# Convolution blocks of 49 tiles instead of 56, three slots instead of two, and weighing two groups behind picking, in a four-layer graph network

## The reference

```python
# second layer, twice (r0, r1): the weight depends on the edge's type
x_src = x[src]
for r in range(8):
    msg = msg + jnp.where((edge_type == r)[:, None], x_src @ W[r], 0)
agg = segment_sum(msg * norm[:, None], dst)
out = agg + x @ root + bias

# fourth layer, three times (c0, c1, c2): the weight is a sum over 8 edge attributes and a constant
W = (edge_attr @ ew + eb).reshape(E, 16, 16)
agg = segment_sum(einsum('ei,eio->eo', x[src], W), dst)
out = agg + x @ rw + rb
```

## Time and profile before

| | us |
|---|---|
| runs | 14,904.42, 14,911.91, 14,941.55 |
| median | 14,911.91 |
| profiled execution | 14,959.53 |
| its span, first to last instruction | 14,958.3 |
| mean granted TensorE clock (share of full) | 0.744 |
| busy: VectorE / GpSimd / TensorE / ScalarE | 11,150.7 / 9,259.2 / 8,297.6 / 4,791.5 |
| share of the span: VectorE / GpSimd / TensorE / ScalarE | 75% / 62% / 55% / 32% |

### The profile page before, as it was taken

One profiled execution on the slowest core, in us unless ns is written; L12 is line 12 of the kernel. 1 busy time (PEld: TensorE's weight loads), 2 busy tenths in 40 slices (PEclk: granted clock), 3 DMA queues, 4 the chain that ended last, 5 costly groups with the idle time before them and its releaser, 6 DMA issues. The chain is left out here.

```text
span 14958.3 us, 147756 instructions
## 1 busy us (share of the span) xinstructions
PE 8297.6 (55%) x41291; PEld 5702.8 (38%) x41291; DVE 11150.7 (75%) x19230; ACT 4791.5 (32%) x2765; POOL 9259.2 (62%) x6976
## 2 busy tenths in 40 slices
PE   1222222222220688588836566665668858885886
PEld 0111111111110566466623233333356646663664
DVE  6999999999998566466635455554559967995996
ACT  0111111111110466456621001010037746773774
POOL 6777777777752466556655555555337756774776
PEclk5555555555555899789967777787779989997998
DMA  2444444444441222122211111111123323332332
GB/s 83 156 154 153 153 153 156 157 154 153 153 157 40 84 63 67 53 61 67 65 42 36 37 37 34 38 36 37 27 69 114 111 79 100 113 111 67 114 111 73
DMA packets 629773, 1371.10 MB, mean 92 GB/s; under 512 B 262833, under 2 KB 403118, under 8 KB 554126
## 3 DMA queue, kind: packets, MB, share of 16 engines
q1 hardware_dynamic: 405534, 1076.25, 20.0%
q0 software_dynamic: 224112, 293.30, 8.8%
HBM read 656.16 MB, written 712.80 MB: 92 GB/s over the span
## 5 line engine op out<-in xcount | busy, mean ns | idle before, releaser
L536 POOL DMA_INDIRECT h<-in_x,idx x1568 | 3051.7, 1946 | 1206.2 <-DMA efT<-in_edge_attr_t 785.3
L550 PE MATMUL PS<-waug,efT 17*128 17x256 f32 x6272 | 1129.4, 679 | 3167.2 <-DVE e L587 2179.1
L1681 PE MATMUL PS<-hot,lhs 128*128 128x392 bf16 x9408 | 1855.5, 355 | 1228.4 <-issue 762.8
L1668 POOL DMA_INDIRECT myg<-node_table,mix x1568 | 1662.6, 1060 | 1323.1 <-DVE mmsg L1737 797.5
L550 PEld LDWEIGHTS PS<-waug,efT 17*128 17x128 f32 x6272 | 695.2, 313 | 3600.9 <-DVE e L587 2225.8
L1681 PEld LDWEIGHTS PS<-hot,lhs 128*128 128x128 bf16 x9408 | 954.6, 103 | 2129.6 <-issue 1111.2
L1305 PE MATMUL PS<-every_weight,dstf 112*128 112x144 f32 (+1 forms) x8960 | 1313.8, 291 | 493.9 <-DVE dstf L1405 409.0
L1305 PEld LDWEIGHTS PS<-every_weight,dstf 112*128 112x128 f32 x8960 | 1252.3, 197 | 666.4 <-DVE dstf L1405 466.6
L1752 DVE TENSOR_TENSOR lhs<-mkx,m 128x512 bf16<-128x512 bf16 x1176 | 429.5, 421 | 1439.2 <-remote 1092.3
L571 ACT ACTIVATE cf<-cf 128x256 f32<-128x256 f32 x196 | 81.7, 417 | 3843.9 <-DVE e L614 3843.9
L1283 POOL DMA_INDIRECT c0yg<-node_table,c0ix x672 | 859.0, 1278 | 591.7 <-DMA c0ix<-in_src 288.3
(11 more groups left out here) (393 smaller groups left out, 18785.4 us busy)
## 6 DMA issues: line engine op xcount, KB each, us to landing
softmax_maxima<-M SPq DMA_DIRECT2D x196, 1024.0 KB, 8.6
softmax_denominators<-ST SPq DMA_DIRECT2D x196, 1024.0 KB
softmax_numerators<-ST SPq DMA_DIRECT2D x196, 1024.0 KB
r0rb<-pick_b SPq DMA_DIRECT2D x56, 512.0 KB
r0ra<-pick_a SPq DMA_DIRECT2D x56, 512.0 KB
r1rb<-pick_b SPq DMA_DIRECT2D x56, 512.0 KB
r1ra<-pick_a SPq DMA_DIRECT2D x56, 512.0 KB
c0rb<-pick_b SPq DMA_DIRECT2D x56, 512.0 KB
```

The costliest lines, as they stand in the source:

```text
L536: PO.indirect_dma_start(h[b.k][:, q, :], None, io["x"], bass.IndirectOffsetOnAxis(ap=idx[b.k][:, q:q + 1], axis=0))\
L550: mm = PE.matmul(PS[0:CH, 4 * message + 2 * (n % 2) + r, 0:C2], efT[b.k][row:row + D + 1, n // 2, :], waug[row:row + D + 1, C2 * message:C ...
L1668: PO.indirect_dma_start(yg[b.k][:, q, :], None, table8, bass.IndirectOffsetOnAxis(ap=ix[b.k][:, q:q + 1], axis=0))\
L1681: mm = PE.matmul(PS[:, 6 + k, 0:A7 // 2], lhs[(G * b.k + q) % 2][:, r, part, :], hot[4 * ((G * b.k + q) % 2) + r][:, k * A7 // 2:(k + 1) * ...
```

## The change

A block has 49 tiles, so there are 32 blocks. Of these 25 tiles are gathered (before: 24 of 56) and 24 are picked, in 6 groups (before: 8). A convolution thus issues 800 gathers for 672, and works 192 groups for 224. The widened one-hots, the picked rows in PSUM and the masked rows have three slots. TensorE picks a whole group and then weighs the group two steps back; products and the constant's copy come one step later than before. The row loads come in thirds of a block, 1,024 columns each.

```diff
-TBC, NBC = 56, 28
-NG, HG = 24, 8
+TBC, NBC = 49, 32
+NG, HG = 25, 6
...
-            hot_ = [sb(f"{name}hot{k}", [128, KT, 512], F32R, L) for k in TWO]
-            ra = [sb(f"{name}ra{k}", [128, 2048], I16, L) for k in TWO]
-            rb2 = [sb(f"{name}rb{k}", [128, 2048], I16, L) for k in TWO]
-            mx = [dstf[0:A9 * D, 512 * k:512 * k + 512] for k in TWO]
+            hot_ = [sb(f"{name}hot{k}", [128, KT, 512], F32R, L) for k in range(3)]
+            ra = [sb(f"{name}ra{k}", [128, 1024], I16, L) for k in range(3)]
+            rb2 = [sb(f"{name}rb{k}", [128, 1024], I16, L) for k in range(3)]
+            mx = [dstf[0:A9 * D, 512 * k:512 * k + 512] for k in range(3)]
...
                     if more:
                         load_ix(b.on(2))
                         load_low(b.on(2), 0)
+                        load_low(b.on(2), 1)
                     if b.on(-1).exists():
                         store_sums(b.on(-1))
                     if more:
                         load_co(b.on(2))
                         load_high(b.on(2), 0)
-                        load_low(b.on(2), 1)
+                        load_low(b.on(2), 2)
                         load_high(b.on(2), 1)
+                        load_high(b.on(2), 2)
...
                 def pick_rows(b, q, m0, m1):
                     if m0 == 0:
                         PE.wait_ge(*h_cv.at(groups(b, q + 1)))
-                        if due(m := groups(b, q - 1)):
+                        if due(m := groups(b, q - 2)):
                             PE.wait_ge(*h_mk.at(m))
...
                     for q in range(HG):
                         if nx:
-                            pick_rows(nx, q, 0, 9)
-                        if q:
+                            pick_rows(nx, q, 0, 2 * KT)
+                        if q > 1:
                             if nx:
-                                weigh_rows(nx, q - 1)
+                                weigh_rows(nx, q - 2)
                         elif b:
-                            weigh_rows(b, HG - 1)
-                        if nx:
-                            pick_rows(nx, q, 9, 2 * KT)
+                            weigh_rows(b, HG - 2 + q)
...
                 def scale_gathered(b, n):
-                    ts = slice(4 * n, 4 * n + 4)
+                    ts = slice(5 * n, 5 * n + 5)
...
                         one_hots(nx, p, 3)
-                        if p == 0:
+                        if p < 2:
                             if b:
-                                scale_picked(b, HG - 1)
+                                scale_picked(b, HG - 2 + p)
                         elif nx:
-                            scale_picked(nx, p - 1)
-                    if b and not both:
-                        add_typed(b, 8)
-                        add_typed(b, 9)
+                            scale_picked(nx, p - 2)
+                    if b:
+                        if not both:
+                            add_typed(b, 6)
+                        carry_in(b)
+                        by_destination(b)
```

More of the change, by code:

```diff
@@ L1165, in program @@
         c_ix, c_co, c_st = pair("c_ix"), pair("c_co"), pair("c_st")
-        h_ra, h_rb = pair("h_ra"), pair("h_rb")
-        c_ix, c_co, c_st, h_ra, h_rb = ([Since(x) for x in two_] for two_ in (c_ix, c_co, c_st, h_ra, h_rb))
+        c_ix, c_co, c_st = ([Since(x) for x in two_] for two_ in (c_ix, c_co, c_st))
+        h_ra, h_rb = ([Since(sem(f"{n}{j}")) for j in range(3)] for n in ("h_ra", "h_rb"))
         c_sc, c_pr, c_al, c_tr, c_msg = (Since(sem(n)) for n in ("c_sc", "c_pr", "c_al", "c_tr", "c_msg"))
@@ L1181, in conv @@
             Y0 = 0 if both else NG
-            NSC, NTR = (6, 13) if both else (0, 6)
+            NSC, NTR = (5, 11) if both else (0, 5)
             index_c = src_c if both else typed
@@ L1210, in conv_sync, with rows, load_low, load_high @@
             def conv_sync():
[L1211 to L1215, removed]
+                def rows(b, j, from_):
+                    return from_[some(b, NG + 8 * j, 8), :].rearrange("(a t) c -> a (t c)", a=1).to_broadcast([128, 1024])
+                def load_low(b, j):
+                    if due(n := b.on(-1).count(3 * KT, KT * j + KT)):
                         SP.wait_ge(*h_oh.at(n))
                         SP.nop(nofuse=True)
-                    SP.dma_start(rb2[half][:, :], rows(b, half, pick_b)).then_inc(h_rb[half].sem, 16)
-                def load_high(b, half):
-                    if due(n := groups(b.on(-1), 4 * half + 4)):
+                    SP.dma_start(rb2[j][:, :], rows(b, j, pick_b)).then_inc(h_rb[j].sem, 16)
+                def load_high(b, j):
+                    if due(n := groups(b.on(-1), 2 * j + 2)):
                         SP.wait_ge(*h_mk.at(n))
                         SP.nop(nofuse=True)
-                    SP.dma_start(ra[half][:, :], rows(b, half, pick_a)).then_inc(h_ra[half].sem, 16)
+                    SP.dma_start(ra[j][:, :], rows(b, j, pick_a)).then_inc(h_ra[j].sem, 16)
                 def load_ix(b):
@@ L1246, in first @@
                 def first(b):
-                    for half in TWO:
-                        load_low(b, half)
-                        load_high(b, half)
+                    for j in range(3):
+                        load_low(b, j)
                     for k in TWO:
                         load_ix(b.on(k))
+                    for j in range(3):
+                        load_high(b, j)
+                    for k in TWO:
                         load_co(b.on(k))
-                    for half in TWO:
-                        load_low(b.on(1), half)
-                        load_high(b.on(1), half)
+                    for j in range(3):
+                        load_low(b.on(1), j)
+                        load_high(b.on(1), j)
                 def body(b):
@@ L1367, in steps @@
                             keeps(b)
-                        if p and nx:
-                            copy_always(nx, p - 1)
+                        if p > 1 and nx:
+                            copy_always(nx, p - 2)
                 def first(b):
@@ L1386, in one_hot @@
                     if c == 0:
-                        if j % 2 == 0:
-                            V.wait_ge(*h_rb[j // 2].at(b.count(16, 16)))
+                        V.wait_ge(*h_rb[j].at(b.count(16, 16)))
                         if due(n := groups(b, 2 * j - 2)):
                             V.wait_ge(*h_cv.at(n))
-                    V.tensor_scalar(hb[j % 2][:, c, :], rb2[j // 2][:, 1024 * (j % 2):1024 * (j % 2) + 1024], pick[:, c:c + 1], None,
-                                    ALU.is_equal).then_inc(h_oh.sem, 1)
+                    V.tensor_scalar(hb[(3 * b.k + j) % 2][:, c, :], rb2[j][:, :], pick[:, c:c + 1], None, ALU.is_equal)\
+                        .then_inc(h_oh.sem, 1)
                 def one_hots(nx, p, n):
@@ L1399, in mask @@
                 def mask(b, q):
[L1400 to L1401 removed]
+                    if q % 2 == 0:
+                        V.wait_ge(*h_ra[q // 2].at(b.count(16, 16)))
                     V.wait_ge(*h_g.at(groups(b, q + 1)))
[L1403 removed]
+                    if due(n := groups(b, q - 2)):
                         V.wait_ge(*h_sel.at(n))
[L1405 to L1406 removed]
+                    at = 512 * (q % 2)
+                    V.scalar_tensor_tensor(out=mx[q % 3][:, :], in0=ra[q // 2][0:A9 * D, at:at + 512],
+                                           scalar=pick_row[0:A9 * D, 0:1], in1=PS[0:A9 * D, 3 + q % 3, :],
                                            op0=ALU.is_equal, op1=ALU.mult).then_inc(h_mk.sem, 1)
```

83 lines of the change are left out of this document (35 added, 48 removed).

## The result

The changed kernel takes 15,261.7 us (median of 4 runs, 15,244 to 15,271), the kernel before 14,926.5 us beside it (4 runs); the ratio is 1.0224, 95% interval 1.0206 to 1.0243. That is +335 us where +88 were forecast.

The account below looks back on a forecast made before the run. Three engines near 85 to 90% in c1, VectorE and TensorE setting the pace; afterwards the gathers would. c +79 each (+237), r -70 and -80: net +87 us, on 14,911.9 giving 15,000 us, 0.6% slower; range 14,840 to 15,350.

Parts of the forecast that it names:

- The gathers' price: GpSimd, steady blocks: a gather takes 1.224 us in c, a block 38.2; an r block of 25 gathers takes 35.9.
- the gather at 12494.68: Trace row in c1, read as a gather beside a one-hot taking 1.36 us, against 0.94 with VectorE standing still.
- the alternative: GpSimd in c: each of 21 one-hots costs gathers its whole 0.49 us, a block 42.7 us instead of 38.2; not taken.
- Rival C: One-hots stop stretching the gathers: block 32.4 us, c about 105 us and r about 185 shorter each, 14,230 us; chance 0.05.
- The chain hidden behind the gathers: Pick, mask, weigh and product take about 26 to 30 us per block, under GpSimd's 35.9 and 38.2; gain counted at nothing.
- The start: First blocks of each convolution: late release kept, GpSimd then waits about 27 us in r and 30 in c.
- The late release in r: Masks in r blocks start some 9 us late, a wait called "remote"; forecast that GpSimd's wait for messages goes.
- 26 + 9 = 35: r block: rest of the block plus late release, just below the gathers' 35.9 us; passing it would bring Rival B.
- Rival B: r blocks: late release lasts until GpSimd pauses, which waits some 10 us per block; 300 us more each, 15,600; chance 0.12.
- The argument against it: Against Rival B: c has runs of gathers as long and no such stall after its first block.
- The rest of the span: Outside first to last gather of the five convolutions: the tail behind the last gather stays, no change counted.

## Why the prediction was wrong

*The gathers' price.* Right. In c1 the excess over 0.944 us was put at 0.28 and is 0.26; the block at 38.2 and is 37.8; the convolution to the end of its last gather at 1,242.6 us, measured 1,242.7. In r the mean was put at 1.129, and is 1.105 in the steady stretch. Two readings on the way don't hold. The one-hot that the gather at 12494.68 meets is not the one shown above it, which had ended by then, but the next:

```profile
12495.15 0.48 DVE L1391 TENSOR_SCALAR c1hb<-c1rb,pick 128x1024 bf16<-128x1024 int16 x1
```

It ends at 12495.63 and the gather 0.41 us later. That is the pattern: of 428 gathers in c1 before that met one one-hot and no scan, 343 ended some 0.4 or 0.8 us after it. So a gather seems to be held until the one-hot's end, and loses only what is then left of it. The text charged the whole 0.49 us as the alternative (42.7 us per block) and dropped it for the measured 0.28; by these rows being held to the end and a mean loss of 0.28 don't exclude each other. And Rival C's terms add up to some 14,245 us and not 14,230.

*The chain hidden behind the gathers.* Right in c (GpSimd waits for no message in the steady stretch, VectorE for gathers about 5.9 us per block). In r only without the slow issue.

*The start.* Right: GpSimd waits 31.4 us in c1 and 26.6 in r1, put at 30 and 27.

*The late release in r.* **This step failed.** The text took the 9 us stall as a block that stays the same, set 26 + 9 = 35 below the gathers' 35.9 us, and let the wait for messages go. It didn't go: over r1 it is 203.5 us in 30 waits, 26.6 at the start and 6.1 in each other. Those 177 us, less some 30 by which gathers and pauses came out cheaper, are the difference of some 145 us from the forecast of 1,170.6, and the same again in r0. The mistake is one of kind and not of size. The stall has no length of its own: it was some 9 us per block before, some 27 us in every second of the new blocks with two slots (r1 1,445 us), and some 8 us per block with three, and it went with the rate of the gathers. So it could not be carried over into the new block as a constant. It was Rival B in its result, late messages in every block, at 6 us per block where B had 10, and I gave it 0.12; B's condition, that the stall lasts until GpSimd pauses, holds in the changed kernel for only about half of the stalls over 3 us. The argument against it, that c has runs of gathers as long, was the clue misread. In steady c VectorE stands for at most 7.0 us at a time, and a gather beside its work takes up to 1.7 us, so the gathers come less closely. That this is why c is spared is a reading; in r the rate was tested, and it decides.

*The rest of the span.* Counted at nothing, it was 70 us shorter. From one convolution's last gather to the next one's first it is 9 to 12 us less in r0, c0 and c1, as the last blocks are shorter; 40 us lie about the third layer.

Sum: c +231 for +237, r +144 for -150, the rest -70 for 0.

## What to carry to other kernels

Before a stall is called hidden, ask what begins and ends it. One that hangs on what another engine does has no fixed length to put into a sum: here three slots shortened it, and only fewer or slower gathers removed it. When a wait is called "remote", count which instruction should have ended it; the one recorded just before need not be it. A loss in "issue" or "remote" that no row explains may be a condition of the run: take the two kernels' ratio in both conditions before a shape is tuned to one. Here the same change is 2.2% slower with it and 3.4% slower without.

## What the hardware did that was not expected

- While indirect gathers followed each other every 1.25 us, TensorE's finished groups were released late: the mask of a group that ended at 6917.10 started at 6930.46. In the changed kernel TensorE's instructions then also came singly, 0.7 or 1.4 us apart. With gathers about 1.33 us apart late releases came in some blocks, at 1.44 and 1.66 us in none, and with 12 gathers per block in none.
- The same program took 14,911 to 15,016 us in some groups of runs and 13,481 to 13,484 in others, and in the second no mask of r1 or c1 waited for a late release. The convolutions' VectorE instructions took the same to 1%, their matmuls and gathers to 5%.
- A memset of 16 numbers on GpSimd (0.13 us) behind a gather left the gathers 1.26 us apart, for 1.25 without: it lies within the pause of 0.30 us. One of 256 took 391 ns on average beside VectorE's work.
